# An attention and expert layer on one core: keys in halves, value blocks sooner, one transpose and one choice moved

## What is computed

```
x = x + xattn(layernorm(x), ctx)           # 16 heads of 32; q, k, v with bias; scores masked above the diagonal
h = layernorm(x)
qkv = (layer_norm(h) * w + b) @ qkv_weight.T   # 4 groups: 4 q heads, one k and one v head each
h1 = h + attention(q, k, v) @ proj_weight.T
t = layer_norm(h1) * w + b; top 2 of 8 experts by softmax(t @ router_weight)
out = x + h1 + sum over the two of p * gelu(t @ w1[e]) @ w2[e]    # at most 1280 rows per expert
```

## Time and profile before

| | us |
|---|---|
| median of three runs (lowest, highest) | 1589.51 (1587.81, 1590.07) |
| the profiled execution | 1583.6 |
| its span | 1581.8 |
| TensorE busy | 1477.9 |
| VectorE busy | 920.4 |
| GpSimd busy | 833.5 |
| ScalarE busy | 712.1 |

### The profile page before, as it was taken

How to read it: one execution, slowest core, us unless ns; L and a number is a source line. 1 busy time by engine, 2 the same in 40 slices (tenths; PEclk the granted TensorE clock), 3 DMA queues, 4 the chain that set the end, 5 groups by cost and what they waited for, 6 DMA issues and landing times. The chain is left out here.

```text
span 1581.8 us, 31078 instructions
## 1 busy us (share of the span) xinstructions
PE 1477.9 (93%) x11056; PEld 1309.9 (83%) x11057; DVE 920.4 (58%) x1741; ACT 712.1 (45%) x1425; POOL 833.5 (53%) x951
## 2 busy tenths in 40 slices
PE   8798899999999999899859998999999899999986
PEld 6577788888888888788749988998999789899876
DVE  3767677777778767788665464433233653453361
ACT  2445545555555555565415453433233643342341
POOL 2445455556666556698725566542542855354332
PEclk9999999999999999999959999999999999999999
DMA  7212211122222111222223343432422534333222
GB/s 262 66 63 75 88 59 50 63 72 82 75 75 67 62 66 64 75 93 88 99 80 91 78 88 100 104 83 54 107 58 48 135 90 103 81 94 54 32 35 25
DMA packets 64400, 125.96 MB, mean 80 GB/s; under 512 B 13369, under 2 KB 13785, under 8 KB 63724
## 3 DMA queue, kind: packets, MB, share of 16 engines
q1 hardware_dynamic: 45932, 93.81, 18.2%
q0 software_dynamic: 17920, 29.31, 10.9%
q10 hardware_dynamic: 384, 0.61, 0.1%
HBM read 89.14 MB, written 46.27 MB: 86 GB/s over the span
## 5 line engine op out<-in xcount | busy, mean ns | idle before, releaser
L1503 PEld LDWEIGHTS hidden_ps<-gT,w 128*128 128x128 f32 x2880 | 350.3, 192 | 11.3 <-ACT hT L1408 3.9
L1503 PE MATMUL hidden_ps<-gT,w 128*128 128x256 f32 x2880 | 352.9, 284 | 7.0 <-ACT hT L1408 3.5
L1530 PE MATMUL expert_ps<-w,hT 128*128 128x512 f32 x1440 | 341.0, 396 | 8.1 <-DVE og L1458 8.1
L1530 PEld LDWEIGHTS expert_ps<-w,hT 128*128 128x128 f32 x1440 | 271.9, 191 | 65.9 <-DVE og L1458 8.9
L1283 POOL TENSOR_TENSOR w<-raw,w 128x1024 fp32r<-128x1024 f32 x62 | 152.9, 2514 | 261.5 <-ACT w L1277 261.5
L1433 DVE TENSOR_TENSOR hT<-gl,hT 128x512 fp32r<-128x512 f32 x160 | 125.9, 795 | 249.0 <-ACT hT L1408 225.3
L1406 ACT ACTIVATE gl<-hidden_ps 128x512 f32<-128x512 f32 x160 | 95.7, 598 | 326.6 <-PE hidden_ps L1503 258.6
L1387 POOL DMA_INDIRECT out_dram<-og,idx x78 | 126.0, 1616 | 72.8 <-DVE og L1458 44.0
L1458 DVE TENSOR_SCALAR og<-expert_ps,kept 128x512 f32<-128x512 f32 x80 | 59.3, 749 | 156.4 <-PE expert_ps L1530 147.4
L1416 ACT ACTIVATE gT<-yk 128x256 fp32r<-128x256 f32 x160 | 67.0, 419 | 127.7 <-DVE yk L1444 118.7
L1375 POOL DMA_INDIRECT xg<-normed_tokens,idx x78 | 86.4, 1108 | 56.2 <-POOL idx L1370 30.9
(11 more groups left out here) (184 smaller groups left out, 3079.5 us busy)
## 6 DMA issues: line engine op xcount, KB each, us to landing
raw<-L_ffn_moe_w_dram SPq DMA_DIRECT2D x64, 512.0 KB
normed_tokens<-h SPq DMA_DIRECT2D x128, 65.0 KB
xa<-x_dram SPq DMA_DIRECT2D x32, 256.0 KB, 2.7
xc<-x_dram SPq DMA_DIRECT2D x32, 256.0 KB, 3.0
attended_rows<-x SPq DMA_DIRECT2D x32, 256.0 KB, 2.1
fx<-attended_rows SPq DMA_DIRECT2D x128, 64.0 KB
out_dram<-fx SPq DMA_DIRECT2D x128, 64.0 KB
fx<-qkv_rows_dram SPq DMA_DIRECT2D x1, 1536.0 KB, 6.7
```

The lines of the kernel that those rows point to most:

```text
L1503: last = pe.matmul(pH[:, q, f * W:(f + 1) * W], w1[p][l][:, k, cols], xT[g.s % 2][r][:, k, :], start=k == 0 and n == 0, stop=k == KT - 1 a ...
L1530: last = pe.matmul(pY[:, k, :], hT[par][l][:, f, k * P:(k + 1) * P], w2[p][r][:, f, :], start=f == 0 and n == 0, stop=f == FT - 1 and n == 2)
```

## The change

1. Keys: ScalarE copies the high halves of the context's slice (616 columns, into the space of wqkv) and of the key weights' (512, into that of wpj), VectorE subtracts the low halves, and TensorE makes three passes over eight products per slice, 96 instructions. The statistics of the first two x tiles stand behind these on VectorE, their normalizing and the copy of wq behind them on ScalarE. The weights of proj are now split first, those of qkv after.
2. Values: the table `VALUES` gives block 0 ahead of the first q and block 1 ahead of the first scores in step 2, block 2 in step 3, block 3 at the head of step 4 and block 4 ahead of the scores in it, in banks 4, 5, 4, 6, 5. VectorE's biases and SyncE's copies follow the table.
3. A job other than scores that takes bank 0 or 1 from the scores waits for the first half of pr only.
4. Up to step 38 (`LATE`) VectorE turns q ahead of the second softmax's sums.
5. On odd steps 5 to 13 ScalarE copies the turned shares ahead of the x tile's high half, and VectorE makes that tile's low half behind the sums of the exponentials.
6. The choice of tiles 26 to 30 is made in step 49, behind the gap of the logits; piece 7's low half is left to POOL in the experts' part.

```diff
@@ -164,9 +164,11 @@
-LATE_LOW = {LATE + 11: 6, LATE + 12: 7}
+LATE_LOW = {LATE + 11: 6}
...
-CHOICES = {STEPS - 7: (0, 26, 0), STEPS - 6: (0, 26, 1), STEPS - 5: (0, 26, 2), STEPS - 2: (26, 31, None)}
+VALUES = {2: ((0, 0), (1, 2)), 3: ((2, 2),), 4: ((3, -1), (4, 2))}
+VALUE_BANKS = (4, 5, 4, 6, 5)
+CHOICES = {STEPS - 7: (0, 26, 0), STEPS - 6: (0, 26, 1), STEPS - 5: (0, 26, 2), STEPS - 3: (26, 31, None)}
@@ -180,13 +182,16 @@
     fz, fq, fs, fo, ft, fr = (tile(i, FF + n) for n in range(6))
-    jobs = [("xt", tx, 0, 1)] + [("pt", tp, j, 0) for j in range(4)] + [("p2t", fo, 0, 0)]
+    def values(stage):
+        return [("val", b, 0, 1) for b, at in VALUES.get(i, ()) if at == stage]
+
+    jobs = values(-1) + [("xt", tx, 0, 1)] + [("pt", tp, j, 0) for j in range(4)] + [("p2t", fo, 0, 0)]
+    jobs += values(0)
     if i % 2 == 0:
...
     jobs += [("s2", fs, 0, 1), ("o2", fo, 0, 1)]
-    if 0 <= i - 2 < VB:
-        jobs += [("val", i - 2, 0, 1)]
+    jobs += values(2)
     jobs += [("s", tq, 0, 0), ("qkv", fq, 0, 1),
@@ -199,7 +204,9 @@
         return 2
-    if kind in ("pt", "val"):
+    if kind == "val":
+        return VALUE_BANKS[t]
+    if kind == "pt":
         return 4 + j % 2
@@ -343,7 +351,10 @@
             for old, t_old, j_old in ousted[kind, t, j]:
-                pe.wait_ge(*read_out[old](t_old, j_old))
+                if old == "s" and kind != "s" and place[kind, t, j] < 2:
+                    pe.wait_ge(s["shifted"], 2 * t_old + 1)
+                else:
+                    pe.wait_ge(*read_out[old](t_old, j_old))
@@ -383,8 +394,8 @@
             if n < 4:
-                return n, rqkv[:, n, :], [w[:, n, :] for w in wqkv], qkv_in
-            return n, rpj[:, n - 4, :], [w[:, n - 4, :] for w in wpj], pj_in
+                return n, rpj[:, n, :], [w[:, n, :] for w in wpj], pj_in
+            return n, rqkv[:, n - 4, :], [w[:, n - 4, :] for w in wqkv], qkv_in
@@ -413,16 +424,15 @@
                     load_x(i + 2)
-                b = i - 3
-                if 0 <= b < VB:
+                t = tile(i, LP)
+                if t is not None:
+                    need(sp, s["x2_done"], t - 1)
+                    sp.dma_start(xc[:, t % 2, :], x2d[row0(t):row0(t) + P, :]).then_inc(xc_in[t % 2], 16)
+                for b, _ in VALUES.get(i - 1, ()):
                     sp.wait_ge(s["val_done"], b + 1)
...
                           .then_inc(va_in[b], 16)
-                t = tile(i, LP)
-                if t is not None:
-                    need(sp, s["x2_done"], t - 1)
-                    sp.dma_start(xc[:, t % 2, :], x2d[row0(t):row0(t) + P, :]).then_inc(xc_in[t % 2], 16)
                 f = tile(i, FF + 6)
@@ -593,6 +603,10 @@
+            for k in range(KT):
+                act.wait_ge(keys_in[k], 32)
+                act.activation(cTh[0][:, k, :], cT[:, k, :], ACT.Copy)
+                act.activation(wpj[0][:, k, :], rk[:, k, :], ACT.Copy).then_inc(s["key_hi"], 1)
             for t in range(2):
@@ -607,25 +621,31 @@
-            def high_halves(i):
...
+            def normed_high(i):
+
                 t = tile(i, 1)
                 if t is not None:
                     act.wait_ge(s["xt_mm"], t + 1)
...
             for i in range(STEPS):
...
+                turned_first = i % 2 == 1 and LP <= i <= FF
+                if not turned_first:
+                    normed_high(i)
...
+                if turned_first:
+                    normed_high(i)
@@ -844,8 +866,13 @@
-            for t in range(2):
-                stats_x(t)
+            for k in range(KT):
+                dve.wait_ge(s["key_hi"], k + 1)
+                dve.tensor_tensor(cTh[1][:, k, :], cT[:, k, :], cTh[0][:, k, :].bitcast(F32), ALU.subtract)
+                dve.tensor_tensor(wpj[1][:, k, :], rk[:, k, :], wpj[0][:, k, :].bitcast(F32), ALU.subtract)\
+                   .then_inc(s["key_lo"], 1)
+                if k % 2 == 1:
+                    stats_x(k // 2)
             dve.wait_ge(s["wq_hi"], 1)
@@ -899,11 +926,11 @@
                 sooner, later = (low_attended, low_normed) if i % 2 == 0 else (low_normed, low_attended)
+                if i in CHOICES and i < STEPS - 3:
+                    choose(*CHOICES[i])
                 if i in LATE_LOW:
...
                     weights["low"](dve, 0, 0, LATE_LOW[i])
-                if i in CHOICES:
-                    choose(*CHOICES[i])
                 f = tile(i, FF + 4)
@@ -939,8 +966,7 @@
                     dve.transpose(ao, bank("o2", f)).then_inc(s["ao_done"], 1)
-                b = i - 2
-                if 0 <= b < VB:
+                for b, _ in VALUES.get(i, ()):
                     dve.wait_ge(s["val_mm"], b + 1)
@@ -979,7 +1005,7 @@
                 f = tile(i, FF + 2)
-                if f is not None:
+                if f is not None and i > LATE:
                     dve.wait_ge(s["exp2"], f + 1)
@@ -990,6 +1016,14 @@
                     dve.transpose(hq, parts(bank("qkv", f, 0))).then_inc(s["q_turned"], 1)
+                f = tile(i, FF + 2)
+                if f is not None and i <= LATE:
+                    dve.wait_ge(s["exp2"], f + 1)
+                    need(dve, s["shared2"], f - 1)
+                    chained(dve.tensor_reduce(den2[:, :], p2, X, ALU.add))
+                    dve.reciprocal(rec2[:, f % 2, :], den2[:, :]).then_inc(s["rec2_done"], 1)
+                f = tile(i, FF + 1)
+                if f is not None:
                     dve.wait_ge(s["v_kept"], f + 1)
@@ -1007,10 +1041,13 @@
                     stats_f(i)
+                if i in CHOICES and i >= STEPS - 3:
+                    choose(*CHOICES[i])
                 if i <= FF:
...
                         sooner(i + 1)
-                    later(i + 1)
+                    if i % 2 == 1 or not LP <= i + 1 <= FF:
+                        later(i + 1)
                 t = tile(i, -1)
@@ -1025,6 +1062,8 @@
                         dve.reciprocal(rec[:, t % 2, heads], den[:, heads]).then_inc(s["rec_done"], 1)
+                if i % 2 == 0 and LP <= i + 1 <= FF:
+                    later(i + 1)
                 if i > FF:
@@ -1043,6 +1082,18 @@
                 transposes("zt", f, z).then_inc(s["zt_mm"], 1)
+
+            def values(i, stage):
+
+                for b, at in VALUES.get(i, ()):
+                    if at == stage:
+                        pe.wait_ge(wv_in, 16)
+                        bank_free(pe, "val", b)
+                        n = min(P, S * SK - P * b)
+                        for k in range(KT):
+                            last = pe.matmul(bank("val", b)[0:n, :], cT[:, k, P * b:P * b + n], rv[:, k, :],
+                                             start=k == 0, stop=k == KT - 1)
+                        last.then_inc(s["val_mm"], 1)
@@ -1061,17 +1112,22 @@
             for k in range(KT):
-                pe.wait_ge(keys_in[k], 32)
-                for n in range(8):
-                    m, h = divmod(n, 2)
-                    last = pe.matmul(bank("key", n)[:, 0:HC], rk[:, k, m * P:(m + 1) * P], cT[:, k, h * HC:(h + 1) * HC],
-                                     start=k == 0, stop=k == KT - 1)
-                    if k == KT - 1:
-                        last.then_inc(s["key_mm"], 1)
+                pe.wait_ge(s["key_hi"], k + 1)
+                for n_pass, (w, c) in enumerate(PASSES):
+                    if n_pass == 1:
+                        pe.wait_ge(s["key_lo"], k + 1)
+                    for n in range(8):
+                        m, h = divmod(n, 2)
+                        final = k == KT - 1 and n_pass == 2
+                        last = pe.matmul(bank("key", n)[:, 0:HC], wpj[w][:, k, m * P:(m + 1) * P],
+                                         cTh[c][:, k, h * HC:(h + 1) * HC], start=k == 0 and n_pass == 0, stop=final)
+                        if final:
+                            last.then_inc(s["key_mm"], 1)
             pe.wait_ge(small_in, 16)
...
                 fz, fq, fs, fo, ft, fr = (tile(i, FF + n) for n in range(6))
+                values(i, -1)
                 if tx is not None:
@@ -1086,6 +1142,7 @@
                     transposes("p2t", fo, p2.rearrange("p b k -> p (b k)")).then_inc(s["p2t_mm"], 1)
+                values(i, 0)
                 if i % 2 == 0 and tq is not None:
@@ -1127,15 +1184,7 @@
                     count_places(*COUNTS[i])
-                b = i - 2
-                if 0 <= b < VB:
-                    pe.wait_ge(wv_in, 16)
-                    bank_free(pe, "val", b)
-                    n = min(P, S * SK - P * b)
-                    for k in range(KT):
-                        last = pe.matmul(bank("val", b)[0:n, :], cT[:, k, P * b:P * b + n], rv[:, k, :],
-                                         start=k == 0, stop=k == KT - 1)
-                    last.then_inc(s["val_mm"], 1)
+                values(i, 2)
                 if tq is not None:
@@ -1387,6 +1436,8 @@
                                                 compute_op=ALU.add).then_inc(scattered[k], 16)
```

(3 more changed lines are left out.)

14 lines of the change are left out of this document (7 added, 7 removed).

## The result

The changed kernel takes 1594.11 us (median of 7 runs, 1592.95 to 1597.14) against 1588.07 (7 runs, 1585.10 to 1590.35) before: ratio 1.0038, 95% interval 1.0028 to 1.0049. It is 6.0 us slower; the forecast was 1585.8, in a range of 1577 to 1594. The profiled executions lie at 1583.6 and 1595.18. The one before is 4.5 under its median and the one after 1.1 over, so the traces stand 11.6 us apart where the kernels stand 6.0.

What follows compares the result with a forecast made beforehand. TensorE, busy for 93% of the span, was taken as the bound. Terms 10.5 - 3 - 8.5 - 2.7 = -3.7 us gave 1579.9 against the profiled 1583.6, so 1585.8 for the median; range 1577 to 1594.

Steps and rivals of the forecast that it cites:

- the gain of steps 5 to 14: Opening's later steps: q waits only for pr's first half, pT copies go ahead of xT_hi; -3 us (none to 5).
- the low half given to POOL: Experts' part: POOL idles 8.63 us before 838.81, with room for 2.5 us; if late, up to 2.5 us lost.
- The stall at the biases: Opening: VectorE's second bias waits for copies behind a load on SyncE, until about 45.2 us; called the largest term.
- the second stall: Opening: block 4's bias waits for its buffer until about 75.8 us, oT_lo behind it; first output projection at 80.2.
- 58.9 for the second q: Opening: start of the second q in us, against 50.41 before with two blocks fewer behind it; a loss of 1.3.
- the forecast's own limits: Opening: the forecast falls if tile 5's transposes come before 83 or after 90 us; expected at 85.3.
- The clock: Opening: each of three new TensorE idles (3.7, 5.0, 6.2 us) lowers the clock, about 1.6 us apiece; +3.5 to +4.
- 1.6 us of idle leave it up: Opening: after 1.58 us of TensorE idle, at 26.47, q did not run at the lower clock.
- Opening in all: Opening: +6.5 us plus 4 for the clock, +10.5; from below +4, from above +13.
- The turn of q: Steady steps: the values' wait of 0.6 us goes in all 15 steps that show it; -8.5 us (-7 to -9.1).
- The choice a step sooner: End of the main stage: choices made a step earlier, TensorE's 3.09 us wait for them goes; -2.7 us (-1.5 to -3).
- Rival B: Opening +13, half the turn's 9.1 kept, steps 5 to 14 nothing: +5.8, some 1595; 0.18 together with VectorE-paced steady steps.

Runs made afterwards that it cites:

- b: Changed kernel with the copies of the value blocks ahead of the loads of x and xc on SyncE: 1577.53 us, 0.9931 of before.
- l: g without the half release of banks 0 and 1 and without the new odd-step order on ScalarE and VectorE: 1569.81 us, 0.9899 of before.
- d: Kernel before with only the turn of q moved ahead of the second softmax's sums, up to step 38: 1579.71 us, 0.9943 of before.
- c: Changed kernel with piece 7's low half back on VectorE in step 50, the choice staying in step 49: 1593.87 us, 1.0029 of before.
- h: Changed kernel with POOL's low half of piece 7 as four instructions of 256 columns instead of one of 1024: 1593.08 us, 1.0033 of before.
- g: Changed kernel with value copies first on SyncE, piece 7's low half on VectorE and block 0 in bank 2: 1573.48 us, 0.9894 of before.
- k: g with 32 tiny unused matmuls (64 more TensorE instructions) ahead of value block 1: 1565.88 us, 0.9866 of before.
- j: Kernel before with 32 tiny unused matmuls (64 more TensorE instructions) ahead of value block 0: 1592.33 us, 1.0027 of before.
- e: Kernel before with the three-pass keys alone, all other parts of the change undone: 1591.02 us, 1.0021 of before.

## Why the prediction was wrong

Slower instead of faster: the sum was -3.7 and came out as +6.0. Four steps of it failed: the price of the stalls and of the clock in the opening (+10.5, measured 12.3 to 13.5), the gain of steps 5 to 14 (-3, measured none), the low half given to POOL, taken as free (-2.7, measured +1.6), and the experts' loops, which the sum left at nothing (some 5 us between the traces with and without 64 instructions more). The landmarks add up to the 11.6 us of the two traces: 12.3 - 1.3 - 9.4 + 2.7 + 1.6 + 5.7; 5.6 of the 11.6 are the distance of these executions from their medians. Term by term:

- **The stall at the biases: right, and too small.** The order on SyncE was read correctly, and b proves it. Sized wrong was the copy's landing: I took 2.0 us from a transfer of another tensor, so that from the first issue to the bias my numbers give 2.9 us (0.9 and 2.0); it was 5.0 (43.60 to 48.65), and 4.5 at the second stall (76.60 to 81.06). That and the first block's slow 5.37 us made 48.65 of 45.2, and 81.06 of 75.8. My 58.9 for the second q was also 0.3 too much by its own terms (50.4 + 8.94 - 0.7). In the second stall I named oT_lo as what TensorE would wait for; it was the bank: pT's second group takes bank 5 from block 4 and waits for the bias itself (L1139 <- fx). Tile 5's transposes came at 92.22; the forecast's own limits were 83 and 90.
- **The clock: right, and too cheap.** Three falls, at 0.50 to 0.60. I gave 1.6 us to each. They took about 2.1 (the block 5.37 against 3.60, q 6.17 against 5.81), 2.2 (scores 2.00 against 1.13, the block 4.95 against 3.60) and 3.2 (twelve turns of pT 2.99 against some 1.6, the output projection 4.70 against 2.84). Less the 1.4 of before that is 6.1 us against my 4 (and 3 x 1.6 - 1.4 would have been 3.4). My statement that 1.6 us of idle leave it up does not hold everywhere: in d it fell (0.72 from 664 to 668 us) behind an idle of 1.60, though not behind two others of 1.54 and 1.62 just before.
- **Opening in all:** +10.5 forecast; measured +13.5 at tile 5's transposes (92.22 against 78.75, just over the upper bound of 13), +12.9 at tile 2's values and +12.3 at tile 10's.
- **Steps 5 to 14: wrong.** -3 forecast; l shows none that can be measured. I priced the waits that go and not the one that comes in their place, the weighted values' wait for xT_lo.
- **The turn of q: right.** -8.5 forecast, -9.4 in the trace (tiles 14 to 29), -9.1 in the median of d.
- **The choice a step sooner: half right.** The last wait for a choice ends 2.5 us sooner after the last transposes, near the 2.7 forecast, and TensorE's gather of the first expert's tokens starts 3.4 us sooner after them (29.9 against 33.4). But POOL's low half took 2.8 of that (c and h), and the low clock that both kernels have in this stretch ended later (granted clock 0.50 from 831 to 836 us, where it was 0.90 before); from the transposes to the first second product it is +1.6 instead of -2.7. I had asked only whether POOL had time (it had 8.63 us), not what VectorE was doing then. The section of the Trainium skill named above (SBUF — State Buffer, "SBUF: two separate sides") states a lock of this kind, and I did not draw on it.
- **Not in the sum at all:** the place of the experts' loops in TensorE's instructions, 3.4 us of waits, a fall of the clock behind them, and in the experts' part of the traces 5.7 us. In the medians it shows as 4.4 us (g against k) and at most 4.3 (j, whose trace loses 2.9 already up to the last transposes). No row of before could have shown that 64 instructions more would hit it; the 1.7 us of waits without releaser at the loops' heads was the place to look.
- **Open:** between tile 31's values (625) and the last transposes (791) the changed kernel loses 2.7 us. 1.3 of it are two waits for VectorE near 705 (0.4 and 0.9). About 1 is the clock: behind a wait of 3.0 us that both kernels have, it was granted 0.50 and 0.73 from 776 to 784 us, and before 0.62 and 0.96 from 773 to 781. j loses 3.3 there, with nothing changed but the padding, and e nothing. So it is not the change's edits by themselves; what tips it was not found.

Rival B had the right sign and nearly the size (+5.8). Two of its reasons came true, the opening near 13 and nothing from steps 5 to 14. The third did not: the half of the turn's gain that it gave up stayed. That its number fits is luck, since a loss behind the main stage that it did not know stood in for that half. Where I chose wrongly was in giving the opening's and the end's unknowns a mean near their cheap side.

## What to carry to other kernels

Before work is moved ahead, read the queue of the engine that carries its result away: here the copies behind a load cost more than all the rest, and moving them ahead of it turned +6 into -11 us. When an instruction is given to an idle engine, look at what its neighbour on the same memory ports does in these microseconds, and cut it short if it must stand there. If a kernel has loops behind unrolled code, compare the waits without releaser at the loops' heads, and the clock behind them, before an edit is judged by 5 us.

## What the hardware showed that I had not expected

- A VectorE subtraction of two SBUF operands (0.42 us alone) was held until the POOL instruction it met ended: it took 3.07 us against one of 2.35, and two of them about 0.8 us longer than usual against quarters of 0.79.
- 64 instructions more ahead of a loop on TensorE made the part with the loops some 5 us longer in the traces (730.7 to 734.3 us against 725.9 to 728.4; waits of 3.9 to 5.3 us against 1.7 to 2.0, and a lower clock behind them); 128 more cost nothing (726.9).
- Copies of 77 rows and fewer from one buffer of the core to another released their waiter 4.5 to 6.0 us after the first of two or three was issued (43.60 to 48.65, 62.28 to 68.24, 76.60 to 81.06).
- TensorE's clock fell once behind an idle of only 1.60 us, and twice did not behind idles of that length.
